# Sparse attention stage of an eight-batch block: the first two batches' keys and values ahead of their top queries, and the first batch's context and output behind the second batch's values

## What is computed

```python
# third layer, b = 8, l = 1024, 16 heads of 16, TOP_U = 35
q = _split_heads(x @ Wq.T + bq); k = _split_heads(x @ Wk.T + bk); v = _split_heads(x @ Wv.T + bv)
scores_sample = jnp.einsum('bhqd,bhsd->bhqs', q, k_sample) * scale
m = scores_sample.max(axis=-1) - scores_sample.mean(axis=-1)
_, top_idx = jax.lax.top_k(m, TOP_U)
context = jnp.broadcast_to(v.mean(axis=-2, keepdims=True), (b, NHEAD, l, D_HEAD))
q_top = jnp.take_along_axis(q, top_idx[..., None], axis=2)
attn = jax.nn.softmax(jnp.einsum('bhud,bhkd->bhuk', q_top, k) * scale, axis=-1)
out_top = jnp.einsum('bhuk,bhkd->bhud', attn, v)
context = context.at[bi, hi, top_idx].set(out_top)
out = context.transpose(0, 2, 1, 3).reshape(b, l, d) @ Wo.T + bo
# then x = x + layernorm(out), and the feed-forward of the fourth layer on layernorm(x):
y = jax.nn.silu(hf @ w1 + fc1_bias); z = y @ w2 + fc2_bias; x = x + layernorm(h_in + 0.5 * z)
```

## Time and profile before

| what | value |
|---|---|
| median of 3 executions | 2808.05 us (2806.64 to 2810.58) |
| the profiled execution, its own time | 2809.61 us |
| its span in the trace | 2807.8 us |
| PE busy | 2508.2 us, 89% of the span |
| DVE / ACT / POOL busy | 1740.4 / 1181.2 / 895.0 us |
| mean granted TensorE clock | 0.953 of full |

### The profile page before, as it was taken

How to read it: one execution, slowest core, us unless ns; L and a number is a source line. 1 busy time by engine, 2 the same in 40 slices (tenths; PEclk the granted TensorE clock), 3 DMA queues, 4 the chain that set the end, 5 groups by cost and what they waited for, 6 DMA issues and landing times. The chain is left out here.

```text
span 2807.8 us, 40487 instructions
## 1 busy us (share of the span) xinstructions
PE 2508.2 (89%) x14196; PEld 1490.5 (53%) x14196; DVE 1740.4 (62%) x4778; ACT 1181.2 (42%) x1885; POOL 895.0 (32%) x1420
## 2 busy tenths in 40 slices
PE   5999999999999999999718999965899999999997
PEld 2444444454444444344317888743666665666664
DVE  6767676776757678778758664636554444454442
ACT  2556666656656665556513332111232222322321
POOL 4140623517062351612231221114215315234242
PEclk8899999999999999999857999988999999999999
DMA  5252340515334051432120222321102111111010
GB/s 172 61 159 55 124 135 25 183 53 174 85 118 140 25 186 51 152 92 81 47 88 21 76 99 82 129 76 61 46 16 77 31 46 61 31 60 47 16 45 30
DMA packets 150139, 228.64 MB, mean 81 GB/s; under 512 B 18757, under 2 KB 114961, under 8 KB 141650
## 3 DMA queue, kind: packets, MB, share of 16 engines
q1 hardware_dynamic: 145842, 222.04, 25.5%
q0 software_dynamic: 4096, 4.01, 0.5%
HBM read 113.75 MB, written 112.27 MB: 80 GB/s over the span
## 5 line engine op out<-in xcount | busy, mean ns | idle before, releaser
L1109 ACT ACTIVATE pt<-ps 128x1024 f32<-128x1024 f32 (+3 forms) x768 | 600.4, 811 | 306.7 <-PE ps L1005 211.8
L893 DVE CUSTOM_DVE_ANT_0 masked<-ps,mask_q 128x128 bf16<-128x128 f32 (+3 forms) x1024 | 472.9, 485 | 184.4 <-PE ps L981 182.2
L981 PE MATMUL ps<-sk,sq 96*128 96x512 bf16 (+3 forms) x1536 | 430.1, 338 | 57.6 <-DVE mx L893 16.5
L1002 PE MATMUL ps<-sq,sk 99*128 99x512 bf16 (+3 forms) x1536 | 399.5, 329 | 12.3 <-DMA sq<-scratch_nm_parts 10.2
L897 DVE TENSOR_REDUCE mx<-ps 128x1 f32<-128x512 f32 x512 | 351.5, 687 | 92.9 <-PE ps L981 92.4
L981 PEld LDWEIGHTS ps<-sk,sq 96*128 96x128 bf16 x1536 | 132.4, 97 | 377.1 <-DVE mx L893 99.4
L1021 PE MATMUL ps<-pt,val 128*32 128x512 f32 (+3 forms) x3072 | 328.2, 499 | 3.1 <-ACT yt L1117 3.1
L1002 PEld LDWEIGHTS ps<-sq,sk 99*128 99x128 bf16 x1536 | 147.5, 98 | 157.5 <-ACT pt L1109 55.9
L2329 PE MATMUL ps<-w_fc,eyb 128*128 128x256 f32 x1024 | 227.2, 380 | 2.3 <-ACT eyb L2383 2.3
L2317 PE MATMUL ps<-eht,w_fc 128*128 128x512 f32 x512 | 223.1, 594 | 1.7 <-ACT eht L2373 1.7
L2383 ACT ACTIVATE eyb<-ps,w_fc_b 128x512 f32<-128x512 f32 x128 | 88.0, 687 | 303.1 <-PE ps L2317 302.5
(11 more groups left out here) (338 smaller groups left out, 4330.2 us busy)
## 6 DMA issues: line engine op xcount, KB each, us to landing
scratch_stacks<-space SPq DMA_DIRECT2D x32, 768.0 KB, 4.3
sq<-scratch_stacks SPq DMA_DIRECT2D x32, 768.0 KB, 8.8
sk<-scratch_stacks SPq DMA_DIRECT2D x32, 768.0 KB, 9.6
scratch_stacks<-space SPq DMA_DIRECT2D x32, 512.0 KB, 5.0
scratch_x<-xr SPq DMA_DIRECT2D x16, 1024.0 KB, 7.8
space<-in_L_attn_x SPq DMA_DIRECT2D x8, 1024.0 KB, 14.0
scratch_stacks<-space SPq DMA_DIRECT2D x32, 256.0 KB, 5.5
xr<-in_L_attn_x SPq DMA_DIRECT2D x8, 1024.0 KB, 6.3
```

Of the source, the lines that this page charges most:

```text
L893: nc.vector.tensor_tensor_reduce(mem["masked"][:, slot, 0:n], ps[:, RING[slot], 0:n], mem["mask_q"][:, BANK - n:BANK], 1.0, -3e38, ALU.add ...
L981: nc.tensor.matmul(ps[:, bank, 0:n], sq[0:ROWS, h, i * P:(i + 1) * P], sk[0:ROWS, h, half * BANK:half * BANK + n], start=True, stop=True)\
L1002: last = nc.tensor.matmul(ps[:, bank, 0:n], sk[0:ROWS_M, h, j * P:(j + 1) * P], sq[0:ROWS_M, h, q0:q0 + n], start=True, stop=not diag)
L1109: nc.scalar.activation(pt[:, u % 3, 2 * pair:2 * pair + 2, 0:n], ps[:, bank:bank + 2, 0:n], ACT.Exp, scale=SCALE).then_inc(e["exp_done"], 1)
```

## The change

`prob_order` gets a constant `QUERIES_LATE = 2`. For batches 0 and 1, `qx` stands behind `v` instead of ahead of `kt`. Batch 0's `cxt` and `wo` leave the end of turn 0 and stand in turn 1 behind `qx(1)`, ahead of `s(1)`. Batch 0's `a_norm`, `x3_stat` and `hn` go in turn 1 beside the scores and turned weights of batch 1, where before the first two stood at the end of turn 0 and `hn` beside `v(1)`. On PE the waits follow the new neighbours. Nothing is computed that was not computed before, and the lists of SP and POOL keep their order, since their parts of the moved steps stand to each other as they stood.

```diff
--- before.py
+++ after.py
@@ -1861,6 +1861,9 @@
     return out
 
 
+QUERIES_LATE = 2
+
+
 def prob_order():
 
     tiles = range(NT)
@@ -1874,13 +1877,22 @@
         attention, forward, late = t < B, 0 < t <= B, t > 1
         if attention:
             order += [("load_xnt", b + 1)] if b + 1 < B else []
-            order += [("qx", b)] + of(b, "kt", range(KC), range(NHALF)) + [("xm", b), ("base", b)]
-            order += mixed(of(b, "v", tiles), of(f, "hn", tiles) if forward else [])
+
+
+            order += [("qx", b)] if b >= QUERIES_LATE else []
+            order += of(b, "kt", range(KC), range(NHALF)) + [("xm", b), ("base", b)]
+            order += mixed(of(b, "v", tiles), of(f, "hn", tiles) if t > 1 else [])
+            order += [("qx", b)] if b < QUERIES_LATE else []
+            if t == 1:
+                order += of(0, "cxt", range(NHALF), range(KC)) + of(0, "wo", tiles)
             scores = of(b, "s", range(2))
             for mt in range(MT):
                 scores += of(b, "s", [mt + 2]) if mt + 2 < MT else []
                 scores += of(b, "pt", [mt])
-            order += scores[0:2] + mixed(scores[2:], of(p, "f2", range(4, NT)) if late else [])
+            beside = of(p, "f2", range(4, NT)) if late else []
+            if t == 1:
+                beside = of(0, "a_norm", tiles) + of(0, "x3_stat", tiles) + of(0, "hn", tiles)
+            order += scores[0:2] + mixed(scores[2:], beside)
             order += of(b, "ot", range(KC)) + [("fold", b), ("scatter", b), ("load_ctx", b)]
             order += of(0, "dequant", range(4)) + of(1, "round", range(2)) if t == 0 else []
             order += [("rows", 1)] if t == 2 else []
@@ -1894,12 +1906,12 @@
             order += of(p, "r_norm", tiles) + [("store", p)]
         if attention:
             order += [("load_x", b)]
-        if attention:
+        if attention and t:
             order += of(b, "cxt", range(NHALF), range(KC)) + of(b, "wo", tiles)
         if forward:
             order += of(f, "f2", range(4))
-        order += mixed(of(f, "f1", [1], range(F2T)) if forward else [("rest", b)],
-                       of(b, "a_norm", tiles) + of(b, "x3_stat", tiles) if attention else [])
+            order += mixed(of(f, "f1", [1], range(F2T)),
+                           of(b, "a_norm", tiles) + of(b, "x3_stat", tiles) if attention else [])
     return order
 
 
@@ -2203,7 +2215,9 @@
                 kind, b, a = step[0], step[1], step[2:]
                 if kind == "qx":
                     pe.wait_ge(e["spread_ready"], b + 1)
-                    if b:
+                    if b < QUERIES_LATE:
+                        pe.wait_ge(e["v_ready"], NT * (b + 1))
+                    else:
                         pe.wait_ge(e["rows_ready"], b)
                     for n, (mt, k) in enumerate(BLOCKS):
                         last = nc.tensor.transpose(ps[:, 4 + k, n % SIDE * MR:(n % SIDE + 1) * MR],
@@ -2223,7 +2237,7 @@
                     last.then_inc(e["kt_full"], 1)
                 elif kind == "base":
                     pe.wait_ge(e["xm_ready"], b + 1)
-                    if b:
+                    if b > 1:
                         pe.wait_ge(e["att_ready"], NT * b)
                     for k in range(KC):
                         last = nc.tensor.matmul(ps[:, 2, 0:C], xmr[:, k, :], w["ps_wv"][:, k, :],
@@ -2231,8 +2245,11 @@
                     last.then_inc(e["base_full"], 1)
                 elif kind == "v":
                     j, = a
-                    if j < 2:
+                    if j < 2 and b >= QUERIES_LATE:
                         pe.wait_ge(e["qbd_ready"], KC * b + j + 1)
+                    elif j < 2:
+                        if b:
+                            pe.wait_ge(e["rows_ready"], b)
                     else:
                         pe.wait_ge(e["v_ready"], NT * b + j - 1)
                     for k in range(KC):
@@ -2242,8 +2259,12 @@
                 elif kind == "s":
                     mt, = a
                     pe.wait_ge(e["kt_ready"], KC * NHALF * (b + 1))
+                    if b < QUERIES_LATE and mt == 0:
+                        pe.wait_ge(e["qbd_ready"], KC * (b + 1))
                     if mt == 1:
                         pe.wait_ge(e["base_ready"], b + 1)
+                        if b == 1:
+                            pe.wait_ge(e["att_ready"], NT * b)
                     elif mt >= 2:
                         pe.wait_ge(e["exp_ready"], MT * b + mt - 1)
                     cs = chunks_of(mt)
@@ -2282,6 +2303,10 @@
                     last.then_inc(e["fold_full"], 1)
                 elif kind == "cxt":
                     n, k = a
+                    if b == 0 and n == 0:
+                        pe.wait_ge(e["kt_ready"], 2 * NHALF * KC)
+                    elif b == 0:
+                        pe.wait_ge(e["qbd_ready"], 2 * KC)
                     pe.wait_ge(e["ctx_in"][n], 16 * (b + 1))
                     if n:
                         pe.wait_ge(e["rows_ready"], b + 1)
@@ -2289,6 +2314,8 @@
                 elif kind == "wo":
                     j, = a
                     pe.wait_ge(e["cxt_ready"], NHALF * KC * b + KC * (j // 4 + 1))
+                    if b == 0 and j < 2:
+                        pe.wait_ge(e["base_ready"], 2)
                     if j >= 2:
                         pe.wait_ge(e["att_ready"], NT * b + j - 1)
                     for k in range(KC):
```

## The result

| | before | the change |
|---|---|---|
| median of the first comparison | 2809.32 us (4 runs) | 2791.76 us (4 runs, 2790.09 to 2798.61) |
| ratio to before, 95% interval | | 0.9944 (0.9932 to 0.9956) |
| again, beside e5 and e6 (below) | 2810.71 us (11 runs) | 2796.24 us (6 runs), ratio 0.9948 (0.9935 to 0.9961) |
| profiled execution, its own time / its span | 2809.61 / 2807.8 us | 2798.61 / 2796.6 us |

The change makes the kernel faster by 0.56% in the first comparison, 15.7 us of 2809 (12.4 to 19.1 by the interval), and by 0.52%, 14.6 us (11.0 to 18.3), in the second. The forecast was 14.2 us less, 2793.9 us.

A forecast was written before the change was run, and what follows sets the result against it. PE, busy 89% of the span, was taken as the bound, so reordering wins only where it stands still. 8.3 + 16.4 - 10.5 = 14.2 us off 2808.05 gave 2793.9 us, range 2789 to 2801.

The forecast's parts named there:

- The start: Batch 0, up to `s(0)`: PE begins `kt` instead of waiting for `qx`; 8.3 us won, ends 7.3 and 9.6.
- C: Rival at batch 0's start: the start is not freed, 5.9 us left, 2802.2; sign: first `kt` past 1841; chance 0.05.
- The middle: From `fold(0)` to `s(1)`: 41.2 us instead of 57.6, 16.4 won, ends 14 and 18.
- the new wait: On PE before `base(1)`: waits 11.3 us for `xm(1)`, which stands behind `dequant` and two rounds of picking on DVE.
- The lower end, 14: From `fold(0)` to `s(1)`: 14 us won if the clock rises as late as in batch 0 and `eqx(1)` is 3 us late.
- Batch 1's scores: From `s(1)` to `ot(1)`: DVE becomes the bound, 33.2 us instead of 22.7, 10.5 lost, ends 7.8 and 13.
- the walk: DVE's steps beside batch 1's scores: no stop from the third maximum until 5.1 us for POOL's chain before `hn(0)`.
- rival B: Beside batch 1's scores: eight `a_norm` cost 0.40 us each instead of 0.64, 1.9 less, 2792.0; chance 0.16.
- Behind it: After `ot(1)`: every engine's list is as before and nothing waits for a fixed time, so the shift stays to the end.
- The sum: Whole kernel: 8.3 + 16.4 - 10.5 = 14.2 us less, 2793.9 us; chance 0.62.
- Rival A: Beside batch 1's scores: DVE's walk grows by 6 us more, 8.2 us won, 2799.9; chance 0.13.
- D: Before `qx(1)`: waits for batch 1's gather, beside `base(1)`'s 1 MB store; slower from 16.1 us late; chance 0.04.

The follow-up runs named there:

- e5: The change with `dequant` ahead of `ot(0)`, `xm(1)` between its halves, picking in turns 1 and 2, `cxt(0)` and six `wo(0)` ahead of `qx(1)`: 2780.14 us.
- e6: The change with the edits of e5 and e3 together: 2774.70 us, ratio 0.9866 to before.
- e1: The kernel before with only `qx(0)` moved behind `v(0)`, batch 1 as before: 2800.97 us, ratio 0.9964 to before.
- e3: The change with the eight `hn(0)` moved behind batch 1's scores: 2787.36 us, ratio 0.9910 to before.
- e4: The change with `xm(1)` moved ahead of `ot(0)` on DVE: 2794.04 us, ratio 0.9936 to before.

## Why the prediction was right, point by point

**The start.** Predicted 8.3 us, measured 34.4 - 26.0 = 8.4. The parts are as laid out: 0.61 us of waiting for DVE's last `v`, 1.44 from `qx(0)` to `s(0)`. PE began 6.4 us after Z where `exnt` had been seen 6.7 after it. Read by the clock of the trace, the sign named for C did appear, a first `kt` past 1841 (it came at 1842.59); but the whole stage began 2.72 us later in this execution, and from Z the start was on time. That the two numbers agree to 0.1 us is luck: among the seven kernels with this list Z to `s(0)` is 24.9 to 26.7 us. Of `ot(0)` I took no shift. Measured was 10.38 against 9.32, within the -1.0 to +1.6 laid aside for it, and part of that came back in the turned weights ahead of it; 7.8 us were left at F.

**The middle.** Predicted 16.4, measured 57.6 - 42.5 = 15.1. `kt(1)` behind the fold, the new wait (11.3 predicted, 11.39 measured), `eqx(1)` ready in time (POOL was done at 1921.96, F + 27.3, predicted 27.4), `cxt` and `wo` without a bracket ahead of them: each held. The term mis-sized is "`base` and `v` took 9.38 with such a cold start". In the change it is 1924.72 - 1913.78 = 10.9, from `base` to where `qx` could have gone on without its bracket. The clock rose later. Stretches of the change, and then of before (length, busy PE, PEld, DVE, ACT, POOL with counts, clock, DMA share, GB/s):

```profile
1914.00:1916.00 2.00, 2.00 (x5) 1.63 (x6) 0.11 (x1) 0.00 (x0) 0.38 (x1) 0.50 1.10 344
1916.00:1918.00 2.00, 2.00 (x6) 1.56 (x5) 0.72 (x2) 0.00 (x0) 0.00 (x0) 0.50 1.13 373
1918.00:1920.00 2.00, 2.00 (x6) 1.61 (x6) 0.45 (x2) 0.00 (x0) 0.40 (x1) 0.58 0.97 390
1920.00:1922.00 2.00, 2.00 (x11) 1.73 (x11) 0.85 (x2) 0.00 (x0) 1.96 (x1) 1.00 1.08 386
```

```profile
1948.00:1950.00 2.00, 2.00 (x5) 1.64 (x6) 0.00 (x0) 0.00 (x0) 1.86 (x2) 0.50 0.02 4
1950.00:1952.00 2.00, 2.00 (x9) 1.63 (x8) 0.93 (x3) 0.00 (x0) 0.24 (x2) 0.74 0.29 97
```

Before, 1.2 GHz held for 3.1 us after `base(1)` began at 1947.96; in the change for 5.9 us after 1913.78. Half of the difference, 1.4 us, is the miss. It need not come from the change: in e1, with the list and the 8.26 us stop of before, the low clock held for 5.4 us, and `base` and `v` took 10.5. The lower end, 14, had this in it.

**Batch 1's scores.** Predicted 10.5 us lost, measured 31.8 - 22.7 = 9.1. Every step of the walk is there: no gap on DVE from the third maximum at S + 8.5, the last statistic at S + 22.8 (24.0 predicted), 5.06 us for POOL's chain, two `hn`, a copy, and 2.54 us from the last turning to `ot(1)`. (The prediction's terms add to 33.1 and 10.4 as they stand, not 33.2 and 10.5.) The term mis-sized is `a_norm`: the eight took 1.46 + 2.03 + 0.73 = 4.2 us between the scores, not 5.14 as in the earlier trace rows. That is rival B, and about half of what B gave it (0.9 of 1.9 us); 0.3 more were won on the maxima, copies and statistics. The first three took 0.49 each, the next three, in the middle of POOL's adds, 0.68, and the last two, begun behind a maximum when POOL stood idle, 0.37, like an `hn` in the earlier trace rows. The Trainium skill, "SBUF — State Buffer", section "Who interferes with whom", has such an operation and GpSimd shut each other out of shared ports, whichever comes second having to wait; these durations go that way. No run here took POOL's adds away to show that they are the cause.

**Behind it** the shift stayed: 13.7 us at `qx(2)`, and 13.9 at the end of the span (960.4 us after Z against 974.3). The `cxt` at 2008.56, which the prediction cites for "from turn 2 on", lies in turn 1; nothing rests on that.

**The sum.** 8.4 - 0.6 + 15.1 - 9.1 = 13.8 in place of 14.2: two misses of 1.3 and 1.4 us went against each other. The mechanism was right at every step, but a sum that fits to 0.4 us, when its terms move by 1 to 2 us from one execution to the next, is in part luck. Rival A (a walk 6 us longer) and C (the start not freed) did not come; D neither, as `base(1)`'s store beside the gather changed nothing: 5.21 us against 5.34 in the earlier trace rows.

What the prediction left unsaid is more than what it had wrong. It counted DVE's wait before `hn(0)` as a cost and didn't ask what it would be behind the scores: e3 gives 8.6 us between S and `ot(1)` for moving a line. And it named `xm(1)`'s place as what holds `base(1)`, where e4 shows that two more stood close behind it, one on DVE's queue and one on POOL's `eqx(1)`.

## What to carry to other kernels

When a step with a wait is put between the steps of another chain on an engine in order, price the wait of that step as part of the chain, and look for the nearest place where the engine idles anyway: here under `ot(1)`, about 9 us better for the same work. A bracket names the last release and not the ones close behind it; before paying to remove one, read the waiting engine's list to the next two waits, as e4 shows (11.4 us removed, 1.7 won) and e5 (DVE's queue cleared, and POOL's scatter with it: 16 won).

## What the runs showed that I had not expected

- DVE's unpacking of weights (`dequant`) held POOL's first scatter instruction for 4.7 us: 5.68 us beside it, 1.00 us when it was moved (e5). Picking moved too there, but in the change the scatters that ran beside picking took 0.93 to 0.95 us each. In every kernel batch 1's first scatter, beside eight normalisations of DVE (2.70 us, L2187 in the change's list), took 2.24 or 2.25 us. The wait for the context, 17.76 us, which I read as the way over POOL's scatter and the load, was a quarter DVE's.
- With 16 foreign steps beside batch 1's scores, and no wait among them, the scores took 23.2 us (e3) and 23.8 (e6), against 22.7 (before) and 21.9 (e1) with none: 0.5 to 1.9 us for steps that in the prediction's row took 9.6.
- The clock's rise behind the same 8.3 us stop of PE, with the same list, came 3.1 us after work began in one kernel (before) and 5.4 in another (e1). It moved terms of this sum by 1 to 1.5 us, with no change of what runs there.
